# Edge phases of a graph network: source numbers in SBUF, 16-bit types loaded in pairs, two engine programs written out

## The reference, cut to what matters

```python
m = x[src] * rel[edge_type]
m = concatenate([m[:half] @ W_in, m[half:] @ W_out])
deg = segment_sum(ones, dst);  norm = 1 / maximum(deg, 1)
agg = segment_sum(m * norm[dst][:, None], dst)
x = x + res * tanh(agg + x @ W_loop + b)
```

## Time and profile before

| what | value |
|---|---|
| median of 3 runs | 3154.2 us (3149.99 to 3161.88) |
| span of the profiled execution | 3778.1 us |
| setup, from the start | 89 us |
| edge phase of layer 0 | 89 to 1603 us |
| dense phase of layer 0 | 1603 to 1746 us |
| edge phase of layer 1 | 1746 to 3205 us |
| dense phase of layer 1 and experts | 3205 to 3778 us |
| busy share: PE, DVE, ACT, POOL | 81%, 57%, 50%, 55% |
| granted TensorE clock, mean | 0.88 |
| DMA, mean | 111 GB/s |

### The profile page before, as it was taken

One profiled execution on the slowest core, in us unless ns is written; L12 is line 12 of the kernel. 1 busy time (PEld: TensorE's weight loads), 2 busy tenths in 40 slices (PEclk: granted clock), 3 DMA queues, 4 the chain that ended last, 5 costly groups with the idle time before them and its releaser, 6 DMA issues. The chain is left out here.

```text
span 3778.1 us, 69660 instructions
## 1 busy us (share of the span) xinstructions
PE 3050.9 (81%) x20820; PEld 2821.4 (75%) x20820; DVE 2162.4 (57%) x3619; ACT 1896.5 (50%) x3333; POOL 2061.6 (55%) x2028
## 2 busy tenths in 40 slices
PE   2788878888888888787888888888887887676998
PEld 1777777777777777687777777777777777665998
DVE  5555455555555555595555555555555555897566
ACT  5455444545445454475555554545555454444444
POOL 3665555655555555455565565656555564575222
PEclk9888888888888889898898888888888888898999
DMA  7333333434334333244344344444443443333122
GB/s 223 115 114 107 109 105 109 119 110 110 106 110 109 108 109 112 86 142 139 106 120 117 110 120 113 116 109 117 114 114 108 114 113 89 110 111 106 59 73 66
DMA packets 252838, 419.91 MB, mean 111 GB/s; under 512 B 70960, under 2 KB 132848, under 8 KB 252784
## 3 DMA queue, kind: packets, MB, share of 16 engines
q0 software_dynamic: 79872, 218.21, 20.2%
q1 hardware_dynamic: 171984, 200.20, 18.2%
q10 hardware_dynamic: 928, 0.85, 0.1%
HBM read 373.21 MB, written 45.88 MB: 111 GB/s over the span
## 5 line engine op out<-in xcount | busy, mean ns | idle before, releaser
L592 PE MATMUL edge_rg<-edge_rel_hi,edge_hot 128*128 128x256 f32 x6656 | 1719.0, 314 | 146.6 <-issue 129.4
L592 PE MATMUL edge_rg<-edge_rel_lo,edge_hot 128*128 128x256 f32 x4992 | 1425.0, 307 | 101.9 <-issue 98.8
L592 PEld LDWEIGHTS edge_rg<-edge_rel_hi,edge_hot 128*128 128x128 f32 x6656 | 1330.7, 214 | 207.2 <-issue 160.0
L430 POOL DMA_INDIRECT edge_xg<-emb,edge_src_i x832 | 860.8, 1035 | 634.5 <-DVE edge_m_lo L513 371.6
L430 POOL DMA_INDIRECT edge_xg<-h,edge_src_i x832 | 849.5, 1021 | 606.4 <-DVE edge_m_lo L513 355.4
L592 PEld LDWEIGHTS edge_rg<-edge_rel_lo,edge_hot 128*128 128x128 f32 x4992 | 1076.4, 216 | 137.8 <-issue 136.7
L498 DVE TENSOR_SCALAR edge_hot<-edge_typ,type_of 128x512 fp32r<-128x512 int32 x832 | 375.1, 493 | 1123.7 <-remote 760.0
L468 ACT COPY edge_sums_sb<-edge_sums 64x258 f32<-64x258 f32 x416 | 153.2, 368 | 1441.0 <-remote 868.1
L605 PE MATMUL edge_sums<-edge_m_hi,edge_sel 128*128 128x258 f32 x1664 | 495.0, 323 | 267.3 <-issue 211.7
L605 PEld LDWEIGHTS edge_sums<-edge_m_hi,edge_sel 128*128 128x128 f32 x1664 | 359.9, 216 | 312.9 <-issue 312.5
L456 ACT ACTIVATE edge_hot<-edge_typ,minus_type 128x512 fp32r<-128x512 int32 x832 | 555.4, 716 | 42.0 <-remote 15.6
(11 more groups left out here) (157 smaller groups left out, 3721.5 us busy)
## 6 DMA issues: line engine op xcount, KB each, us to landing
edge_typ<-in_edge_type SPq DMA_DIRECT2D x416, 256.0 KB
edge_xg<-emb,edge_src_i POOLq DMA_INDIRECT x832
edge_xg<-h,edge_src_i POOLq DMA_INDIRECT x832
set_x_rows<-in_x SPq DMA_DIRECT2D x25, 256.0 KB
emb<-set_e_rows SPq DMA_DIRECT2D x25, 256.0 KB, 3.5
emb_t<-set_e_t SPq DMA_DIRECT2D x25, 256.0 KB, 2.9
dense_prev<-emb_t SPq DMA_DIRECT2D x25, 256.0 KB, 2.7
h_t<-dense_work SPq DMA_DIRECT2D x25, 256.0 KB, 2.0
```

Source lines behind the costliest of these rows:

```text
L430: pool.indirect_dma_start(xg[:, t, :], None, nodes, bass.IndirectOffsetOnAxis(ap=at, axis=0)).then_inc(gathered[q], 16)
L592: ins = pe.matmul(rg[q % 2][:, t, :], hot[:, q % 2, c, t * P:(t + 1) * P], part[:, c, :], start=(c == 0 and part is rel_hi), stop=(c == FULL))
```

## The change

Four things:

1. The source numbers of all tiles lie in one SBUF tensor `K["src"]` (128 x 832 int32), loaded once in setup. SyncE loads none in the edge phases, GpSimd waits for none, and an indirect DMA takes its column from there. The host lays them out accordingly.
2. Setup loads the types (416 KB), VectorE casts them to int16, and ScalarE stores four copies of them to a DRAM tensor `types_16` (208 KB each). In the edge phases SyncE loads the types for two groups at once, in four DMAs of 32 partitions each, one from each copy; `typ` holds two such pairs, four groups in all. A pair waits only for the one-hot parts of the group that is three before its first.
3. The programs of GpSimd and SyncE in the edge phases are written out for all 52 turns (`rolled=False`); the other three engines keep their loops. The wait for the slot stands as a plain `wait_past` ahead of the gathers.
4. `sel` holds the four 64-column blocks of a group side by side with 64 zero columns behind them; a matmul still takes 128 columns, of which the last 64 are now the next tile's. The result's rows 64 to 127 aren't read, before and after.

```diff
+COPIES = 4
+SHARE = P // COPIES
+PAIR = 2 * GROUP * P
@@ phase_setup
             sp.dma_start(dst_i[:], dst_tiles).then_inc(dst_in, 16)
+            sp.dma_start(types_i[:], types.rearrange("(p k) -> p k", p=P)).then_inc(types_in, 16)
             sp.dma_start(K["res"][:], res.partition_broadcast(P)).then_inc(res_in, 16)
+            sp.dma_start(K["src"][:], src_tiles).then_inc(src_in, 16)
...
             over_chunks(sp, (0, load), (3, store), ring=BUFS)
             sp.wait_ge(res_in, 16)
+            sp.wait_ge(src_in, 16)
+            sp.wait_ge(types_out, 16 * COPIES)
...
             dve.tensor_copy(K["dst"][:], dst_i[:]).then_inc(chain, 1)
+            dve.wait_ge(types_in, 16)
+            dve.tensor_copy(types_h[:], types_i[:]).then_inc(types_cast, 1)
...
+            act.wait_ge(types_cast, 1)
+            for r in range(COPIES):
+                act.dma_start(types_16[ds(r, 1)].rearrange("o (p k) -> p (o k)", p=P), types_h[:]).then_inc(types_out, 16)
             act.wait_ge(consts, 8)
             over_chunks(act, (0, copy), (0, clear), ring=BUFS)
@@ over_groups
-    for i in range(2):
+    apart = 2 if rolled else STEPS
+    for i in range(apart):
         for q in range(GROUPS_IN_RING):
             turn(i, q)
-    with eng.Fori(2, STEPS) as i:
-        for q in range(GROUPS_IN_RING):
-            turn(i, q)
+    if rolled:
+        with eng.Fori(apart, STEPS) as i:
+            for q in range(GROUPS_IN_RING):
+                turn(i, q)
@@ phase_edges
-        typ = s.sb("typ", [P, 2, GROUP * P], I32)
+        typ = s.sb("typ", [P, GROUPS_IN_RING // 2, 2, GROUP * P], I16)
-        sel = s.sb("sel", [P, RING, P], F32R)
+        sel = s.sb("sel", [P, GROUPS_IN_RING, (GROUP + 1) * WIN], F32R)
-        src_i = s.sb("src_i", [P, 2, RING // 2], I32)
...
                 if q % 2 == 0:
-                    for k in (q, q + 1):
-                        wait_past(sp, gathered[k], 16 * GROUP * i)
-                    sp.dma_start(src_i[:, q // 2], src_idx[ds(2 * i + q // 2, 1)].rearrange("o p k -> p (o k)"))\
-                      .then_inc(src_in[q // 2], 16)
-                wait_past(sp, hot_done, g - 1)
-                wait_past(sp, hot_act, g - 1)
-                sp.dma_start(typ[:, q % 2], types[ds(g * GROUP * P, GROUP * P)].partition_broadcast(P))\
-                  .then_inc(typ_in[q % 2], 16)
+                    wait_past(sp, hot_done, g + 2 - GROUPS_IN_RING)
+                    wait_past(sp, hot_act, g + 2 - GROUPS_IN_RING)
+                    for r in range(COPIES):
+                        sp.dma_start(typ[r * SHARE:(r + 1) * SHARE, q // 2].rearrange("p a e -> p (a e)"),
+                                     types[ds(r, 1), ds(g * GROUP * P, PAIR)].rearrange("o e -> (o e)").partition_broadcast(SHARE))\
+                          .then_inc(typ_in[q // 2], 16)
...
-                wait_apart(pool, lo_done, g + 1 - GROUPS_IN_RING, passed)
-                if q % 2 == 0:
-                    wait_apart(pool, src_in[q // 2], 16 * (i + 1), passed)
-                for t in range(GROUP * q, GROUP * (q + 1)):
-                    at = src_i[:, t // (RING // 2), t % (RING // 2):t % (RING // 2) + 1]
-                    pool.indirect_dma_start(xg[:, t, :], None, nodes,
+                wait_past(pool, lo_done, g + 1 - GROUPS_IN_RING)
+                for t in range(GROUP):
+                    at = K["src"][:, GROUP * g + t:GROUP * g + t + 1]
+                    pool.indirect_dma_start(xg[:, GROUP * q + t, :], None, nodes,
                                             bass.IndirectOffsetOnAxis(ap=at, axis=0)).then_inc(gathered[q], 16)
...
-                act.wait_ge(typ_in[q % 2], 16 * ((2 * i + q // 2) + 1))
+                act.wait_ge(typ_in[q // 2], 16 * COPIES * (i + 1))
...
-                    act.activation(hot[:, q % 2, c], typ[:, q % 2], ACT.Abs,
+                    act.activation(hot[:, q % 2, c], typ[:, q // 2, q % 2], ACT.Abs,
...
-                    select(sel[:, GROUP * q:GROUP * (q + 1), 0:WIN],
+                    select(sel[:, q, 0:GROUP * WIN].rearrange("p (t n) -> p t n", n=WIN),
...
-                        lhs = sel[:, GROUP * q + t, :]
+                        lhs = sel[:, q, t * WIN:t * WIN + P]
```

More of the change, by code:

```diff
@@ L22 @@
 I32 = mybir.dt.int32
+I16 = mybir.dt.int16
 U32 = mybir.dt.uint32
@@ L138, in product, with phase_setup @@
     return pe.matmul(out, a[0], b[0], start=False, stop=last)
-def phase_setup(nc, K, x, dst_tiles, res, emb, emb_t):
+def phase_setup(nc, K, x, dst_tiles, src_tiles, res, emb, emb_t, types, types_16):
     with ExitStack() as ctx:
@@ L146, in phase_setup @@
         neg = s.sb("neg", [P, TILES])
+        types_i = s.sb("types_i", [P, TILES], I32)
+        types_h = s.sb("types_h", [P, TILES], I16)
         real = s.sb("real", [P, TILES])
@@ L164, in phase_setup @@
         dst_in = s.sem("dst_in")
+        types_in = s.sem("types_in")
+        types_cast = s.sem("types_cast")
+        types_out = s.sem("types_out")
         res_in = s.sem("res_in")
+        src_in = s.sem("src_in")
         consts = s.sem("consts")
@@ L334, in turn, with phase_edges @@
                 stage(g, (q - lag) % GROUPS_IN_RING, step)
-    for i in range(2):
+    apart = 2 if rolled else STEPS
+    for i in range(apart):
         for q in range(GROUPS_IN_RING):
             turn(i, q)
-    with eng.Fori(2, STEPS) as i:
-        for q in range(GROUPS_IN_RING):
-            turn(i, q)
+    if rolled:
+        with eng.Fori(apart, STEPS) as i:
+            for q in range(GROUPS_IN_RING):
+                turn(i, q)
     for t in range(max(lag for lag, _ in stages)):
         turn(STEPS + t // GROUPS_IN_RING, t % GROUPS_IN_RING)
-def phase_edges(nc, K, layer, nodes, rel, src_idx, types):
+def phase_edges(nc, K, layer, nodes, rel, types):
     first = layer == 0
@@ L375, in phase_edges @@
         rel_split = s.sem("rel_split")
-        src_in = [s.sem(f"src_in{b}") for b in range(2)]
-        typ_in = [s.sem(f"typ_in{b}") for b in range(2)]
+        typ_in = [s.sem(f"typ_in{b}") for b in range(GROUPS_IN_RING // 2)]
         gathered = [s.sem(f"gathered{q}") for q in range(GROUPS_IN_RING)]
@@ L492, in one_hot @@
             def one_hot(g, q, i):
-                dve.wait_ge(typ_in[q % 2], 16 * ((2 * i + q // 2) + 1))
+                dve.wait_ge(typ_in[q // 2], 16 * COPIES * (i + 1))
                 wait_past(dve, rel_done, g - 1)
                 for c in range(HOT_ACT, RCHUNKS):
-                    ins = dve.tensor_scalar(hot[:, q % 2, c], typ[:, q % 2], K["type_of"][:, c:c + 1], None,
+                    ins = dve.tensor_scalar(hot[:, q % 2, c], typ[:, q // 2, q % 2], K["type_of"][:, c:c + 1], None,
                                             ALU.is_equal)
@@ L546, in add_window @@
                     add(q % 2, base, acc_at, acc_added, deg_added)
-                over_groups(dve, (0, one_hot), (1, one_window), (2, message), (5, add_window), (3, low))
+                over_groups(dve, (0, one_hot), (1, one_window), (2, message), (5, add_window), (3, low), rolled=True)
             def long():
@@ L565, in all_windows @@
                         dve.wait_ge(win_step, g * (2 * WINDOWS + 1) + 2 * w + 3)
-                        select(sel[:, GROUP * q:GROUP * (q + 1), 0:WIN], shifted[:]).then_inc(win_selected, 1)
+                        select(sel[:, q, 0:GROUP * WIN].rearrange("p (t n) -> p t n", n=WIN), shifted[:]).then_inc(win_selected, 1)
                         dve.wait_ge(win_summed, g * WINDOWS + w + 1)
                         add(0, w * WIN, half_at + w * WIN, win_added, win_deg)
-                over_groups(dve, (0, one_hot), (2, message), (3, low), (3, all_windows))
+                over_groups(dve, (0, one_hot), (2, message), (3, low), (3, all_windows), rolled=True)
                 dve.wait_ge(win_added, GROUPS * WINDOWS + 1)
@@ L624, in turn_over @@
                     ins.then_inc(turned, 1)
[L626 removed]
+                over_groups(pe, (1, relation_rows), (3, one_window), (4, turn_over), rolled=True)
             def long():
@@ L634, in sum_window @@
                                 ins = pe.matmul(sums_t[0][:, k, :], part[:, q % 2, t, k * P:(k + 1) * P],
-                                                sel[:, GROUP * q + t, 0:WIN], start=(part is m_hi and t == 0),
+                                                sel[:, q, t * WIN:(t + 1) * WIN], start=(part is m_hi and t == 0),
                                                 stop=(part is m_lo and t == GROUP - 1))
@@ L638, in sum_window @@
                         for t in range(GROUP):
-                            ins = pe.matmul(sums_t[0][:, DC, :], K["ones_r"][:], sel[:, GROUP * q + t, 0:WIN],
+                            ins = pe.matmul(sums_t[0][:, DC, :], K["ones_r"][:], sel[:, q, t * WIN:(t + 1) * WIN],
                                             start=(t == 0), stop=(t == GROUP - 1))
@@ L1367, in build @@
     x2 = nc.dram_tensor("x2", [NODES_PAD, DIM], F32, kind="Internal").ap()
```

(1 more changed line is left out.)

21 lines of the change are left out of this document (10 added, 11 removed).

## The result

The change makes the kernel slower by 1.4%: the median is 3208.0 us of 4 runs (3189.7 to 3209.8), against 3158.0 of 4 runs of the kernel before beside it (3150.0 to 3167.9), ratio 1.0144 [1.0119, 1.0169]. The forecast was 3152 us, in a range of 3070 to 3205: the time is 3 us above its upper end and 50 us above the kernel before. The profiled execution spans 3207.9 us, so here the profile does stand for an ordinary run.

What follows compares the result with a forecast made beforehand. The prediction took GpSimd's gathers in the edge phases to be close to the bound. Its terms summed as -2 + 0 + 0 - 5 + 5 = -2 us, from 3154 to 3152 us, with a range of 3070 to 3205.

Steps and rivals of the forecast that it cites:

- GpSimd's gathers are close to the bound: Edge phases, ordinary run: GpSimd's floor is 2209 of 2349 us, about 100 us of removable waits left.
- floor of 5.3 us a group: GpSimd, edge phases: gather busy time plus 0.30 us gaps, 2209 us in both layers, highest of three engine floors.
- 140 us above the floor: Edge phases, ordinary run: all that lies above GpSimd's floor, pipeline filling and emptying included.
- the faster rival: Edge phases: waits above GpSimd's floor go; 3059 if all 100 us, 3110 to 3125 if a third to half; chance 0.36.
- that of the types: Type loads, edge phases: buffers already deep enough, removed wait hidden, worth 0; upper bound of the gain -16 us.
- The slower rival: GpSimd, edge phases: `low` collides with 104 more gathers at 0.57 us, +59, giving 3218; collisions or code, chance 0.24.
- Its rule from the Trainium skill: VectorE (two-port mode or two SBUF inputs) and GpSimd instructions reading SBUF shut each other out for a whole instruction.
- The Trainium skill's other rule: Type loads: one transfer over 128 partitions is preferred; four pieces gain nothing and cost issue time, which is covered.
- Source numbers: Layer starts: gathers need not wait for source loads, nothing to -3.4 us in each layer, taken as -2 in all.
- Setup: Setup: two more 416 KB loads and four 208 KB stores, bounds +2 and +9 us, taken as +5.
- the -5: GpSimd's written-out program: a wait at the gather itself shortens slot waits, -9 us in an ordinary run, taken as -5.
- the signs of being wrong: Mean gather off by over 0.05 us, new gaps behind gathers, or starts under 0.6 us after `low` with median under 3138.

Runs made afterwards that it cites:

- old_types: The changed kernel with the old type loads (int32, one DMA a group, two deep), no cast or copies in setup: 3163.8 us, 1.0005 of the kernel before.
- window_late: The changed kernel with VectorE's `one_window` between `message` and `add_window`, so `low` starts later: 3179.1 us, 1.0058 of the kernel before.
- one_dma: The changed kernel with each pair's types loaded by one DMA over 128 partitions from one copy: 3138.9 us, 0.9928 of the kernel before.
- low_psum: The changed kernel with `low` reading its first operand from PSUM, leaving out the right low part of messages: 2979.8 us, 0.9434 of the kernel before.
- before_again: The kernel before, unchanged, run once more for a profile of an ordinary execution: 3154.3 us, 0.9981.

## Why the prediction was wrong

- **The bound was right.** "GpSimd's gathers are close to the bound": GpSimd never waits in an ordinary run, before or after. But the floor of 5.3 us a group took the mean gather of the earlier trace rows, 1.03 us, as given. A free gather is 0.946, so the true floor is 4 x (0.946 + 0.30) = 5.0, and all above it is held time. Of the "140 us above the floor" none was waiting: an ordinary run before holds its gathers 1818.2 - 1664 x 0.946 = 244 us. There was no wait of GpSimd for the faster rival to take. Late types were there as it supposed, behind the sources in SyncE's queue, and cost nothing; the excess that I put down to waits was collisions.
- **The step that failed** is that of the types: "So the buffers are deep enough as they are [...] The removed wait is hidden, worth 0". The wait was read from an execution that wasn't ordinary; in an ordinary one VectorE finds the types late 130 times. The depth was enough all the same: old_types keeps it and has no such wait. And the wait was hidden, as the step says. What failed is the 0: it prices the type part by the waits that it removes, and leaves out that other loads shift when `low` runs against the gathers, which bound the kernel. Taken alone the type part cost 3196.3 - 3154.3 = +42 us (two sessions). In the whole change the gathers' part of the sum, put at nothing, is +48 us. It comes from layer 0, where a gather that meets `low` now starts 0.24 us after it on average and started 0.64 us after it before, and so has more of it to wait for.
- **The slower rival had the mechanism, and its size by luck.** It forecast 3218 for 104 new collisions, in half of the free groups, at 0.57 us each. That the sum came within 10 us is luck: there were no new ones (412 before, 411 after), and no free groups to hit, since `low` met a gather in nearly every group already. A full collision costs up to 1.1 us, not 0.57: the earlier trace rows had a `low` that had been running for 0.53 us already. And before wasn't free of them: 0.60 us a group in layer 0 (912.2 - 787.1 = 125 us over 208), 0.94 after, and in layer 1 0.57 before, 0.46 after. +70 us and -22 us make the +48. I gave it 0.24 because "the same shift may as well take collisions away"; I didn't ask whether the phase would hold itself once both were timed from the same event.
- **Its rule from the Trainium skill** ("SBUF — State Buffer", "SBUF: two separate sides") says that whichever of the two instructions starts first holds the ports for its whole length. window_late shows just that for the gather, at 0.01 us. The other way round the trace agrees only in part: a `low` that came second was hardly held (1.25 us there, 1219 ns on average in the profile after), and a one-hot that came second only where it began some 0.45 to 0.7 us into the gather (last section). The Trainium skill's other rule, one transfer over 128 partitions ("DMA: Bandwidth & Descriptors", "Rules for kernel authors"), was right in direction: one_dma is 69 us faster than the four pieces. It wasn't for issue time, which is hidden as forecast, but for the phase.
- **Small terms.** Source numbers: forecast -2. GpSimd's idle time at the start of layer 1 went from 14.7 to 11.5 us, and its first gather of layer 0 from 96.99 to 91.71; these two, 3.2 and 5.3 us, are nearly all of the table's 9. So the source part and the written-out programs together were worth about what was forecast, -2 and -5, but at the phases' starts; no run separates the two. What the -5 was for, waits for a slot, wasn't there to be shortened. Setup: +5 was wrong; the first types of layer 0 are issued at 90.87 us, at 90.96 before. int16: 0 as forecast (491 and 493 ns). `sel`: 0, by the constant of old_types. Code of the long program: 0, no gap of a new kind.
- **What would have shown it ahead.** The profiled execution was 624 us longer than the median. I used it for durations, which held, but also for who waits for whom, which didn't. From its timeline a free gather (0.95) and the mean (1.03) were both there to be seen, and the difference, 1710.3 - 1664 x 0.946 = 136 us, was the first sign of what the bound is made of. Of the signs of being wrong that the prediction names, the mean gather showed: 1.12 us against its 1.03, though an ordinary run of the kernel before has 1.09 already.

## What to carry to other kernels

Where a floor is made of an engine's mean duration, split it first into the free duration and what other engines add; here the held part was 244 us of the kernel before, and two edits that never touch the bounding engine (halves of an instruction, another place in VectorE's order) gave 5.8% on the changed kernel. A change to loads that the bounding engine never waits for can still cost, since it can move the phase between two engines, and where both are timed from one event the phase can lock: look at one period in the timeline, not at sums. Before reading waits from a profiled execution, hold its span against the median.

## What the runs showed of the hardware

A gather (an indirect DMA of GpSimd, 128 rows of 1 KB) doesn't begin its work while certain VectorE instructions run that started before it. I sorted the 1664 gathers of the profile after by what VectorE was running when the gather started:

| VectorE runs | gathers | gather us, 10 / 50 / 90% | ends after it, median |
|---|---|---|---|
| nothing | 773 | 0.942 / 0.946 / 0.948 | |
| `message` (one operand in PSUM) | 412 | 0.942 / 0.946 / 0.948 | 0.67 |
| `low` (both in SBUF, 1.22 us) | 410 | 1.177 / 1.766 / 1.951 | 0.91 |
| window comparison (both in SBUF, 0.42 us) | 48 | 1.087 / 1.092 / 1.096 | 0.82 |
| one-hot (types in SBUF, 0.49 us for 512 columns) | 14 | 1.067 / 1.156 / 1.232 | 0.82 |

`message` and `low` have the same shape and length; only where an operand lies differs, and low_psum turned `low` from the third line's kind into the second's (390 gathers started beside it, median 0.946). I had expected a contention that shares the time between the two. It is an order instead: the gather's last 0.8 to 0.9 us start when the VectorE instruction ends, whatever is left of that. The one-hot was unexpected too: it has one large operand in SBUF and holds a gather all the same, to 1.25 us at most, 0.30 more than a free one (the gather at 604.42 of the kernel before took 1.19).

In the other direction the two kinds differ. A `low` that starts during a gather takes its 1.22 us as ever (1.25 at most). A one-hot is held by the gather, but only if it starts some 0.45 to 0.7 us into it: in before_again 41 of the 832 take over 0.60 us, up to 0.72, where the median is 0.48, and those that start in a gather's first 0.4 us take 0.49. Here a gather starts at 383.62, the first one-hot of a pair at 383.70 and the second 0.49 us into the gather; the pair takes 1.11 us where others take 0.88:

```profile
383.62 0.95 POOL L430 DMA_INDIRECT edge_xg<-emb,edge_src_i  x1 [0.31 <-issue]
```

```profile
383.70 1.11 DVE L498 TENSOR_SCALAR edge_hot<-edge_typ,type_of 128x512 fp32r<-128x512 int32 x2 [1.21 <-DMA edge_typ<-in_edge_type]
```
